# Moving two-hop transfers of softmax sums and inverses, and the sum ahead of the experts, within a hand-written order for a two-layer transformer block on one Trainium2 core

## The reference, cut to what matters

```python
h = layernorm(x) * (1 + ca) + sa
x = x + ga * attention_causal(h, 16 heads)          # first attention, head width 16
h = layernorm(x) * (1 + cb) + sb
xn = layernorm(h) * ln_g + ln_b
o  = attention_full(xn, 32 heads) @ wo + h          # second attention, head width 8
y  = gelu(o @ w1[e] + b1[e]) @ w2[e] + b2[e]        # expert e: fixed blocks of 256 tokens
x = x + gb * y
```

## Time and profile before

| | |
|---|---|
| median of 3 runs | 1685.79 us (1683.16 to 1689.93) |
| the profiled execution: its own time | 1687.4 us |
| its span, first to last instruction | 1685.7 us |
| PE busy / DVE busy / ACT busy | 1466.6 / 1161.3 / 997.0 us |
| mean granted TensorE clock | 0.946 of full |
| step length in passes 1 to 5 (mean) | 4.1 us |

### The profile page before, as it was taken

How to read it: one execution, slowest core, us unless ns; L and a number is a source line. 1 busy time by engine, 2 the same in 40 slices (tenths; PEclk the granted TensorE clock), 3 DMA queues, 4 the chain that set the end, 5 groups by cost and what they waited for, 6 DMA issues and landing times.

```text
span 1685.7 us, 29723 instructions
## 1 busy us (share of the span) xinstructions
PE 1466.6 (87%) x9637; PEld 613.4 (36%) x9637; DVE 1161.3 (69%) x2891; ACT 997.0 (59%) x2075; POOL 529.3 (31%) x1218
## 2 busy tenths in 40 slices
PE   5785889979988999798997989989997989997987
PEld 4332323323433334243433334333343424343325
DVE  6666689778775787667785777757776588865720
ACT  1252557746765666564765757566675657775761
POOL 4232335235341334214442234413343024311000
PEclk9697989999998999899998999999999999999999
DMA  6751434645254434625444353535436223533211
GB/s 192 201 121 38 133 111 147 152 115 145 88 169 121 149 90 115 180 67 159 117 141 115 92 157 100 160 101 153 112 98 180 79 84 83 162 85 81 83 33 63
DMA packets 158749, 200.96 MB, mean 119 GB/s; under 512 B 24640, under 2 KB 109952, under 8 KB 158600
## 3 DMA queue, kind: packets, MB, share of 16 engines
q1 hardware_dynamic: 152712, 194.69, 41.0%
q10 hardware_dynamic: 5888, 4.37, 0.9%
HBM read 122.25 MB, written 75.58 MB: 117 GB/s over the span
## 4 chain that ended last, share of the span: by engine, by line
PE 57%; DMA 11%; DVE 10%; SPq 8%; ACT 6%; issue 5%; POOL 3%; POOLq 0%; ACTq 0%; DVEq 0%
PE bank_out L1454 13%; PE bank_scores L1435 10%; PE bank_max L1405 7%; PE bank_side L1538 5%; PE bank_side L1368 4%; DVE neg_max L1679 3%; PE bank_max L1522 3%; DMA inverse_T<-inverse 3%; PE bank_side L1378 3%; DMA sums_T<-out_raw 3%; SPq L811 3%; ACT probs L1226 3%; PE bank_side L1503 2%; SPq L997 2%; DMA inverse<-sums_T 2%
## 5 line engine op out<-in xcount | busy, mean ns | idle before, releaser
L1226 ACT ACTIVATE probs<-bank_scores 128x512 f32<-128x512 f32 (+3 forms) x1536 | 752.6, 543 | 400.8 <-PE bank_scores L1435 391.9
L1679 DVE TENSOR_REDUCE neg_max<-bank_max 128x1 f32<-128x512 f32 x1024 | 654.8, 684 | 117.7 <-PE bank_max L1405 116.1
L1405 PE MATMUL bank_max<-k_stack,q_stack 64*128 64x512 bf16 (+3 forms) x2048 | 321.3, 350 | 95.9 <-DVE neg_max L1679 59.0
L1454 PE MATMUL bank_out<-probs,v_tile 128*9 128x512 f32 (+4 forms) x3072 | 370.6, 555 | 6.5 <-ACT out_raw L1241 2.9
L1435 PE MATMUL bank_scores<-q_stack,k_stack 64*128 64x512 bf16 (+3 forms) x2048 | 320.9, 350 | 35.8 <-ACT probs L1226 31.3
L1676 DVE CUSTOM_DVE_ANT_0 bank_max<-bank_max,causal 128x384 f32<-128x384 f32 (+3 forms) x512 | 241.8, 514 | 112.4 <-PE bank_max L1405 110.5
L1435 PEld LDWEIGHTS bank_scores<-q_stack,k_stack 64*128 64x128 bf16 x2048 | 81.1, 94 | 376.7 <-issue 355.1
L1076 POOL CAST max_parts<-max_row 16x128 bf16<-16x128 f32 x96 | 27.9, 291 | 542.1 <-DVE max_row L1690 542.1
L1405 PEld LDWEIGHTS bank_max<-k_stack,q_stack 64*128 64x128 bf16 x2048 | 104.6, 96 | 179.0 <-issue 132.2
L1538 PE MATMUL bank_side<-w_out,hidden_T 128*128 128x256 f32 x512 | 141.4, 402 | 3.1 <-issue 1.1
L1094 POOL TENSOR_SCALAR_AFFINE_SELECT probs<-probs 128x512 f32<-128x512 f32 x128 | 81.6, 638 | 137.7 <-ACT probs L1226 137.6
(11 more groups left out here) (154 smaller groups left out, 1434.3 us busy)
## 6 DMA issues: line engine op xcount, KB each, us to landing
q_stack<-q_parts SPq DMA_DIRECT2D x124, 256.0 KB, 4.4
k_stack<-k_parts SPq DMA_DIRECT2D x122, 192.0 KB, 6.3
out_raw<-out_raw SPq DMA_DIRECT2D x70, 256.0 KB, 2.1
w_in<-in_L_ffn_w_dram SPq DMA_DIRECT2D x16, 1024.0 KB, 5.2
w_out<-in_L_ffn_w_dram SPq DMA_DIRECT2D x16, 1024.0 KB, 6.8
q_parts<-partsq SPq DMA_DIRECT2D x32, 384.0 KB, 3.8
k_parts<-partsk SPq DMA_DIRECT2D x32, 384.0 KB, 3.2
q_parts<-partsq SPq DMA_DIRECT2D x32, 256.0 KB, 3.8
```

Source lines behind the costliest of these rows:

```text
L1226: nc.scalar.activation(probs[s % 2][:, head_at(k), q0:S], region[bank][:, q0:S], ACT.Exp, scale=float(WIDTH[a]) ** -0.5).then_inc(drained[ ...
L1405: ins = pe.matmul(region[to][:, 0:keys], q_stack[buf][rows, at, qt * P:(qt + 1) * P], k_stack[buf][rows, at, 0:keys], start=(i == 0), stop ...
L1454: ins = pe.matmul(outb[32 * k:32 * k + WIDTH[a] + 1, q0:S], v_tile[a][:, kt, g * GROUP + k, :], probs[s % 2][:, k, q0:S], start=(kt == 0), ...
L1679: v.tensor_reduce(dst, region[bank], AX_X, ALU.max).then_inc(drained[bank], 1)
```

## The change

Only numbers in the tables change; no instruction is added or taken away. In pass n:

- A: `load_sums` 18.1 to 19.1, `invert` and `store_inverse` 20.1 to 23.1, `load_inverse` 21.3 to 24.3, `scale_heads` 23.1 to 28.1 (step and place).
- B: 26.1 to 27.1, 28.1 to 30.1, 29.3 to 32.1, 31.3 to 35.1.
- C: 41.3 to 42.1, 43.3 to 45.1, 44.3 to 47.3, 46.1 to step 1.3 of the next pass.
- the stack (n + 1, unit 3) from 40.3 to 42.3, behind C's `load_sums`; `w_out` now stands ahead of that `load_sums`.
- `ffn_sum` of batch n from 46.3 to 48.1 to steps 7.1 to 8.3 of the next pass; `keep_x` from 2.2 to 17.2 of it; `attention_out` and `v` move up by half a step to two steps.

The first pass and the tail are changed in the same sense. In the tail `ffn_sum` of batch 6 and its experts move back by about three steps; the last of them ends where it did.

```diff
 def place_pass(plan, first, n):
...
-    place_units(plan, first, (3, 13, 73, 83), v_items(0, n + 2))
+    place_units(plan, first, (3, 13, 61, 63), v_items(0, n + 2))
...
-    place_units(plan, first, (33, 43, 53, 63), out_items(b))
-    place_units(plan, first, (181, 201, 201, 213, 231), heads_items(n, 1, 0))
-    place_units(plan, first, (261, 281, 281, 293, 313), heads_items(n + 2, 0, 0))
-    place_units(plan, first, (413, 433, 433, 443, 461), heads_items(n, 1, 1))
+    place_units(plan, first, (33, 41, 43, 53), out_items(b))
+    place_units(plan, first, (191, 231, 231, 243, 281), heads_items(n, 1, 0))
+    place_units(plan, first, (271, 301, 301, 321, 351), heads_items(n + 2, 0, 0))
+    place_units(plan, first, (421, 451, 451, 473, 493), heads_items(n, 1, 1))
+    place_units(plan, first, (71, 73), in_pieces("ffn_sum", e, 0))
+    place_units(plan, first, (81, 83), in_pieces("ffn_sum", e, 1))
+    place_units(plan, first, (172,), [("keep_x", n)])
...
-    place_units(plan, first, (21, 83, 163, 251, 323, 403),
+    place_units(plan, first, (21, 83, 163, 251, 323, 423),
                 [("stacks", n + 2, 0), ("stacks", n, 4), ("stacks", n, 5), ("stacks", n + 2, 1), ("stacks", n + 1, 2), ("stacks", n + 1, 3)])
...
-    place_units(plan, first, (463, 471), in_pieces("ffn_sum", n, 0))
-    place_units(plan, first, (473, 481), in_pieces("ffn_sum", n, 1))
-    place_units(plan, first, (471, 502), [("bias_columns", n), ("keep_x", n + 1)])
+    place_units(plan, first, (471,), [("bias_columns", n)])
 def place_first_pass(plan):
...
-    place_at(plan, (73, 81, 81, 89, 97), heads_items(0, 1, 0))
-    place_at(plan, (135, 143, 143, 151, 159), heads_items(0, 1, 1))
-    place_at(plan, (167, 175, 175, 183, 191), heads_items(2, 0, 0))
+    place_at(plan, (74, 91, 91, 102, 121), heads_items(0, 1, 0))
+    place_at(plan, (137, 151, 151, 161, 177), heads_items(0, 1, 1))
+    place_at(plan, (167, 179, 179, 187, 199), heads_items(2, 0, 0))
...
 def place_tail(plan, first):
...
-    place_units(plan, first, (181, 201, 201, 213, 231), heads_items(n, 1, 0))
-    place_units(plan, first, (331, 343, 343, 353, 363), heads_items(n, 1, 1))
-    place_units(plan, first, (61, 61), layernorm_items(b, 1)[:2])
-    place_cluster(plan, first, 63, e, 0, norm_under(b, 1))
+    place_units(plan, first, (191, 231, 231, 242, 281), heads_items(n, 1, 0))
+    place_units(plan, first, (341, 371, 371, 391, 411), heads_items(n, 1, 1))
+    place_units(plan, first, (53, 61), in_pieces("ffn_sum", e, 0))
+    place_units(plan, first, (63, 71), in_pieces("ffn_sum", e, 1))
...
-    place_units(plan, first, (371, 373), in_pieces("ffn_sum", n, 0))
-    place_units(plan, first, (383, 393), in_pieces("ffn_sum", n, 1))
...
-    place_cluster(plan, first, 403, n, 0)
...
+    place_units(plan, first, (413, 421), in_pieces("ffn_sum", n, 0))
+    place_units(plan, first, (423, 431), in_pieces("ffn_sum", n, 1))
...
+    place_cluster(plan, first, 433, n, 0)
...
```

More of the change, by code:

```diff
@@ L352, in place_first_pass @@
     place(plan, n1 + 7, [("keep_v", 1)])
-    place(plan, n1 + 6, [("stacks", 1, 2)])
-    place(plan, n1 + 36, [("stacks", 1, 3)])
+    place(plan, n1 + 10, [("stacks", 1, 2)])
+    place(plan, n1 + 40, [("stacks", 1, 3)])
     place_norm(plan, (138, 140, 142, 144, 144, 144, 144, 150, 152), 3, 0)
-    place(plan, n1 + 37, in_pieces("ffn_sum", 0, 0) + in_pieces("ffn_sum", 0, 1), 2)
-    place(plan, n1 + 54, [("keep_x", 1)])
     place_at(plan, (157, 161), features_items(3, 0))
-    place_at(plan, (173, 175, 177, 179, 181, 183, 185, 189), qk_items(0, 3))
+    place_at(plan, (165, 169, 173, 177, 179, 181, 185, 189), qk_items(0, 3))
     place(plan, 180, [("load_gate", 1)])
@@ L369, in place_tail @@
     place_units(plan, first, (23,), [("head_features", b, 0, 1)])
-    place_units(plan, first, (33, 41, 43, 53), out_items(b))
-    place_units(plan, first, (181, 201, 201, 213, 231), heads_items(n, 1, 0))
-    place_units(plan, first, (331, 343, 343, 353, 363), heads_items(n, 1, 1))
-    place_units(plan, first, (61, 61), layernorm_items(b, 1)[:2])
-    place_cluster(plan, first, 63, e, 0, norm_under(b, 1))
[L375 to L380, removed]
+    place_units(plan, first, (33, 41, 43, 51), out_items(b))
+    place_units(plan, first, (191, 231, 231, 242, 281), heads_items(n, 1, 0))
+    place_units(plan, first, (341, 371, 371, 391, 411), heads_items(n, 1, 1))
+    place_units(plan, first, (53, 61), in_pieces("ffn_sum", e, 0))
+    place_units(plan, first, (63, 71), in_pieces("ffn_sum", e, 1))
+    place_units(plan, first, (152,), [("keep_x", n)])
+    place_units(plan, first, (61, 61), layernorm_items(b, 1)[:2])
+    place_cluster(plan, first, 73, e, 0, norm_under(b, 1))
+    place_units(plan, first, (83, 91), [("ffn_input", b, 0), ("ffn_input", b, 1)])
+    place_expert_out(plan, first, (81, 83, 93, 103), e, 0, 0)
+    place_units(plan, first, (103, 111, 113, 113, 113, 113, 113, 133, 141), layernorm_items(b, 2))
+    place_expert_out(plan, first, (113, 123, 133, 143), e, 0, 1)
+    place_units(plan, first, (93, 152, 153), [("load_expert_in", e, 1), ("store_y", e, 0), ("load_expert_out", e, 1)])
+    place_units(plan, first, (151, 153), features_items(b, 2))
     place_units(plan, first, (11, 83, 201, 243, 323, 403),
                 [("stacks", n, 4), ("stacks", n, 5), *(("stacks", n + 1, u) for u in UNITS[1])])
-    place_units(plan, first, (153, 163, 173, 183, 193, 203, 213, 223), qk_items(1, n + 1))
+    place_units(plan, first, (161, 163, 173, 183, 193, 203, 213, 223), qk_items(1, n + 1))
     place_units(plan, first, (231, 251), features_items(n + 1, 1))
@@ L391, in place_tail @@
     place_units(plan, first, (342, 351, 352), [("store_y", n - 1, 1), ("load_gate", n + 1), ("load_expert_out", n, 0)])
-    place_units(plan, first, (371, 373), in_pieces("ffn_sum", n, 0))
-    place_units(plan, first, (383, 393), in_pieces("ffn_sum", n, 1))
-    place_units(plan, first, (403, 403, 401), [("keep_x", n + 1), ("bias_columns", n), ("bias_part", n + 1, 0)])
-    place_cluster(plan, first, 403, n, 0)
[L396 to L402, removed]
+    place_units(plan, first, (413, 421), in_pieces("ffn_sum", n, 0))
+    place_units(plan, first, (423, 431), in_pieces("ffn_sum", n, 1))
+    place_units(plan, first, (442, 433, 433), [("keep_x", n + 1), ("bias_columns", n), ("bias_part", n + 1, 0)])
+    place_cluster(plan, first, 433, n, 0)
+    place_units(plan, first, (451,), [("load_expert_in", n, 1)])
+    place_expert_out(plan, first, (441, 443, 453, 463), n, 0, 0)
+    place_expert_out(plan, first, (473, 483, 493, 503), n, 0, 1)
+    place_units(plan, first, (512, 513), [("store_y", n, 0), ("load_expert_out", n, 1)])
+    place_cluster(plan, first, 523, n, 1)
+    place_units(plan, first, (551,), [("load_expert_in", n + 1, 0)])
+    place_expert_out(plan, first, (531, 533, 543, 553), n, 1, 0)
     place_expert_out(plan, first, (563, 573, 583, 593), n, 1, 1)
-    place_units(plan, first, (541, 602, 603), [("bias_columns", n + 1), ("store_y", n, 1), ("load_expert_out", n + 1, 0)])
+    place_units(plan, first, (571, 602, 603), [("bias_columns", n + 1), ("store_y", n, 1), ("load_expert_out", n + 1, 0)])
     place_last_experts(plan, n + 1, SLOTS * (first + 2 * T_STEPS * HEADS[1] // GROUP) + 3)
```

## The result

| | before | after |
|---|---|---|
| median (lowest to highest), 4 runs each | 1687.12 us (1683.16 to 1689.93) | 1637.38 us (1635.07 to 1640.43) |
| ratio | | 0.9708, 95% interval 0.9679 to 0.9737 |
| profiled execution: time / span | 1687.4 / 1685.7 us | 1635.07 / 1633.3 us |
| mean granted clock | 0.946 | 0.963 |
| pass 3 | 197.7 us | 187.5 us |

The change makes the kernel 2.9% faster, where 5.3% was forecast; the median lies 5 us above the range. The direction was right, the size was not.

The account below looks back on a forecast made before the run. PE was taken as the bound, idling behind late DVE work, with half-clock stretches after. Gains of 66.5 + 27.8 + 4.0 + 11.1 = 109.4 less 19.5 gave -89.9: 1687.4 to 1597.5, median 1596 us, range 1573 to 1632.

Parts of the forecast that it names:

- A: First exchange of passes 1 to 5: its product comes later, all five PE gaps go, -14.1 us.
- B: Second exchange of passes 1 to 5: reciprocal two steps later, about 1 us left each time, -29.4 us.
- C: Third exchange of passes 1 to 5: `load_sums` goes behind `w_out`, sums 1.2 us late each pass, -12 us.
- The later hops are safe: Exchange C: store two steps and more before `load_inverse`, product another two, `ffn_sum` five steps off.
- the forecast's own case: Whole kernel, 1574 to 1606 us, chance 0.62: from the whole 109.4 us gained to 3 us at each B.
- R1: Rival, the wait moves: sums at C land 3 us or more late, clock falls again, 1616 us; chance 0.18.
- `max_rows`, +4 us: `max_rows` at step 45.3 must land before the next pass's first scores; waits of 0.8 us a pass, +4.
- gaps of about 1 us should not lower it: Granted clock: short gaps leave it at full, so the half-clock loss of 27.8 us in passes 1 to 5 goes.
- 15 us, covered: Stack (n + 1, unit 3), behind `w_out` and the sums, goes out 15 us before its first use next pass.
- R4: Rival, slower: the stack (n + 1, unit 3) lands after first use, PE waits; 1700 at 16 to 18 us lateness; chance 0.04.
- R2: Rival: PE is no longer the bound, DVE may set the pace, half the gain goes, 1641 us; chance 0.13.
- W: Rival theory in the follow-up runs: DVE now limits the pass, the gap opens elsewhere, within 5 us of 1637.

Follow-up runs that it names:

- kernel two: The changed kernel with POOL's `bias_part` moved from step 1.3 to step 0.1 and the product left at 1.3: 1604.32 us, ratio 0.9515.
- the best version: The changed kernel with `bias_part` at step 0.1 and the stack (n + 1, unit 3) back at step 40.3: 1592.28 us, ratio 0.943; also called the fastest version.
- the last kernel: The changed kernel with `bias_part` early, the stack at 40.3 and `load_gate` moved from step 42.3 to 46.1: 1596.15 us, ratio 0.9442.
- kernel three: The changed kernel with the two multiplications by the gate left out of POOL's `bias_part`, the product still at its place: 1626.48 us in a single run.

## Why the prediction was right in direction and wrong in size

**The step that failed** is the costing of the moved product at C: "the product another two" steps, under "The later hops are safe". It asked only whether the transfer ahead of the product would have landed, and took the product's length, 0.69 us, from its old place. It did not ask what POOL does at the new place. Of a moved instruction I had counted its inputs and the DMA queue, not the other engine. In the runs the product took 4.8 us beside POOL's `bias_part`, in six places. The price was 33 us, and 1604.2 and 1604.3 us, with the collision taken away from either side, lie within the forecast's own case (1574 to 1606). That they lie so near is in part luck, since the other terms missed in both directions, as follows.

Passes 1 to 5 took 981.5 us before, 933.6 after and 906.4 in kernel two. The forecast had 14.1 + 29.4 + 12.0 + 27.8 less 5.5 added, so 903.7. The part ahead of pass 1 was to give 4.0 us and gave 8.0 (6.2 in kernel two). Tail and end were to give 8.1 us and lost 3.5 (in kernel two they gave 1.0): kernel two ran 15 us there at half clock, the kernel before 10.

**A.** 14.1 us of gaps and their clock were to go. Alone it gave 25.0 us, against 24 expected. Right, and on its reason: the product waits for nothing.

**B.** 29.4 us, about 1 us left each time. `sums_T` waits 5.6 us in all; alone it gave 42.8 us, against some 40 for the gaps and their clock. Right.

**C.** The 1.2 us a pass for sums behind `w_out` did not come (0.32 us, once), and neither did R1. The sums did land with `w_out`: in pass 5 `w_out` landed at 1318.91 and DVE, waiting for the sums, went on at 1319.23. That agrees with the ring order that the Trainium skill states (DMA: Bandwidth & Descriptors, "Queues, rings and completion order"). It cost nothing because `w_out` took only 5.9 to 6.2 us to landing there, not the 6.8 taken, and the reciprocal comes 5.5 to 6.6 us behind the issue of the sums. But C with the ends gave only 18.2 us, where the forecast's 89.9 less 24 for A and 40 for B leaves 26. In the five passes, 973.7 us long in the kernel without A's and B's part, it gave 7.8 us, where 12.0 and 7.7 of clock less 5.5 added make 14.2.

**`max_rows`, +4 us.** This was the right mechanism at the wrong price. The waits rose as forecast, from 4.2 to 8.1 us, but in passes 2 to 5 the longest of them was followed by a half-clock stretch, which I had excluded with "gaps of about 1 us should not lower it". I had taken that from one gap of 1.8 us that left the clock at full. The runs that shorten SP's busy stretch gained 10 to 12 us, with the waits unchanged in sum and the stretches gone. I had also costed the stack's move by its own first use alone ("15 us, covered"), not by who stands behind it on SP. R4, built on that, did not occur.

**R2.** DVE works 145 of 187.5 us in pass 3 after the change, and PE is busier than before: it had not become the bound. W fell for the same reason.

**What would show it.** Right: no DVE wait for `inverse_T` in these passes, `sums_T` at 5 to 12 us (5.6), no PE wait above 0.3 us before `ffn_sum` or L1345. Not met: hardly a half-clock stretch (nine, of 34 us), clock above 0.97 (0.963), a pass of 178 to 182 us (187.5), DMA's share below 5% (6%). In the best version the passes take 177 to 182 us and the clock 0.975: the figures were within reach of this change, less one collision and with the stack left in its place.

Open stays why the clock fell behind some gaps of about 1 us and not behind others, why the end of the program runs 1.3 us at half clock in one kernel and 15 in another with the same instructions there, what lets a product into a POOL train in one meeting and not in another, and whether the change of the gate's load is worth anything.

## What to carry to other kernels

When an instruction is moved in a hand-written order, look at the new place on every engine, not only at its inputs: a DVE operation with both inputs in SBUF can end up beside a train of POOL operations and wait, here for all of it, and the trace shows this as a long instruction, not as idle time. Compare each operation's mean and longest time before and after, first of all where busy time rose with no instruction added. On a queue that issues in order, a moved transfer is to be costed by the small urgent ones that now stand behind it.

## What the runs showed of the hardware that was not expected

**A DVE product can wait for a whole train of POOL operations.** It took 4.76 us beside six, 3.40 beside four and 0.68 beside none. The Trainium skill (SBUF — State Buffer, "Who interferes with whom") says that a DVE instruction with two SBUF inputs contends with a GpSimd instruction that reads SBUF, and this agrees: both inputs of the product lie in SBUF. The `neg_max`, with one input in PSUM, are 1.29 us for two beside the additions of kernel two as elsewhere:

```profile
939.83 1.29 DVE L1681 TENSOR_REDUCE neg_max<-bank_max 128x1 f32<-128x512 f32 x2 [0.92 <-PE bank_max L1407]
```

The Trainium skill also says (same page, "SBUF: two separate sides") that whichever of the two starts first keeps the other out for the whole instruction. The last kernel agrees to the letter: the product waited for the addition that was running, and POOL's next one waited for the product (1.17 in place of 0.72 us). In the changed kernel and in kernel three the rule holds only for the start, for POOL was in an operation when the product began. But the rule speaks of one instruction, and there DVE did not get its turn between POOL's: it waited for that one and for the six (in kernel three, four) that followed back to back. POOL lost nothing there: 1.41 and 2.75 us beside the product, 1.41 and 2.77 us without it. In these twelve meetings the product began 0.1 to 0.2 us before the end of the small operation ahead of the train, in the last kernel in the midst of the train; whether that decides it, no run shows.

**Half-clock stretches behind short gaps.** After the change, PE waits for `max_parts` of 0.90 to 1.34 us were each followed within 1 to 2 us by a stretch at half clock of 3.4 us (as the 0.90 us wait at 956.02 above). In the kernel before, a gap of 1.8 us was not, and in the fastest version waits of up to 1.2 us were not.
